# Second attention of a two-layer gated block: value products one tile behind their transpositions, first scores in front of the last down product

## What is computed

```python
x = x + tanh(g_xattn[0]) * _L0_xattn_ref(_layernorm(x), ctx_1024, W, b)          # phase A, one head
x = x + tanh(g_ffn[0])   * _L0_ffn_ref(_layernorm(x), ...)                       # phase B, 16 experts, top 4, shared expert
x = x + tanh(g_xattn[1]) * _L1_xattn_ref(_layernorm(x), ctx_1024, Wq, Wk, Wv, Wo, ...)   # phase C, 16 heads of 8
x = x + tanh(g_ffn[1])   * _L1_ffn_ref(_layernorm(x), ...)                       # phase D, 8 experts, top 2
...
    scores = jnp.einsum('bhqd,bhkd->bhqk', q, k)
    attn = jax.nn.softmax(scores, axis=-1)
    ctx = jnp.einsum('bhqk,bhkd->bhqd', attn, v)
    return ctx @ Wo.T + bo
```

## Time and profile before

| | |
|---|---|
| median of 3 runs | 322.72 us (322.35 to 323.2) |
| profiled execution, its own time | 322.1 us |
| span of the profile | 320.3 us |
| TensorE clock granted over the span | 0.987 of full speed |
| PE busy | 283.6 us, 89% |
| DVE busy | 237.1 us, 74% |
| ACT busy | 129.9 us, 41% |
| GpSimd busy | 87.7 us, 27% |

### The profile page before, as it was taken

The page is one execution under the profiler, slowest core; times in us unless marked ns, Lnnn a source line. Parts: engine busy times, 40 slices in busy tenths (PEclk is TensorE's granted clock), DMA queues, the critical chain, the costliest instruction groups (busy, mean ns, idle before and its releaser), DMA issues.

```text
span 320.3 us, 5453 instructions
## 1 busy us (share of the span) xinstructions
PE 283.6 (89%) x1646; PEld 210.7 (66%) x1646; DVE 237.1 (74%) x660; ACT 129.9 (41%) x275; POOL 87.7 (27%) x162
## 2 busy tenths in 40 slices
PE   6899689999899799488789789889889999999994
PEld 5688467666476465277677677768676676676661
DVE  2887979769989986557677686686748977778572
ACT  1587533242342332445454554554442332323320
POOL 8475310100650410733175165355110100100000
PEclk9999979999999999889999999999999999999999
DMA  6900164282341430000000000000024053231640
GB/s 225 337 21 0 37 222 148 54 242 67 102 156 46 132 123 33 0 2 0 2 1 2 0 2 3 0 0 3 0 86 158 25 190 75 106 125 35 210 154 33
DMA packets 15066, 25.26 MB, mean 79 GB/s; under 512 B 2341, under 2 KB 4339, under 8 KB 14835
## 3 DMA queue, kind: packets, MB, share of 16 engines
q1 hardware_dynamic: 12968, 23.88, 22.6%
q10 hardware_dynamic: 2072, 1.07, 1.2%
HBM read 22.98 MB, written 1.25 MB: 76 GB/s over the span
## 4 chain that ended last, share of the span: by engine, by line
PE 65%; issue 10%; DVE 9%; ACT 5%; DMA 5%; POOL 3%; SPq 2%; POOLq 0%; DVEq 0%; ACTq 0%
PE S L542 24%; PE Ybank L564 15%; PE Ybank L710 10%; PE S L687 2%; PE Tb L482 2%; DMA CR<-comb_rows 2%; DMA X<-in_x 2%; PE bank L697 2%; DVE xn L1059 2%; DMA comb_rows<-ct 1%; ACT pt L973 1%; PE Tb L674 1%; ACT PX L963 1%; SPq L307 1%; PE bank L580 1%
## 5 line engine op out<-in xcount | busy, mean ns | idle before, releaser
L858 ACT ACTIVATE sg<-S 128x512 f32<-128x512 f32 x64 | 38.0, 596 | 72.5 <-PE S L542 62.6
L1205 DVE TENSOR_TENSOR hb<-sg,CR 128x512 f32<-128x512 f32 x64 | 45.1, 705 | 13.0 <-issue 4.8
L337 POOL TENSOR_TENSOR rstd<-ve,mhalf 128x4 f32<-128x4 f32 x11 | 11.1, 1011 | 134.6 <-DVE ve L1052 134.6
L1198 DVE TENSOR_TENSOR sg<-sg,S 128x512 f32<-128x512 f32 x64 | 43.5, 680 | 5.7 <-ACT sg L858 3.5
L710 PE MATMUL Ybank<-VX,pt 128*128 128x128 f32 (+1 forms) x320 | 39.1, 277 | 6.7 <-ACT pt L973 6.7
L710 PEld LDWEIGHTS Ybank<-VX,pt 128*128 128x128 f32 (+1 forms) x320 | 37.1, 191 | 9.2 <-issue 9.1
L542 PE MATMUL S<-xh,WBH 128*128 128x512 f32 x64 | 33.3, 520 | 5.8 <-DVE sg L1198 3.0
L542 PE MATMUL S<-xh,UPH 128*128 128x512 f32 x64 | 36.1, 565 | 0.0
L564 PE MATMUL Ybank<-hb,W2T 128*128 128x512 f32 x64 | 33.0, 599 | 1.6 <-DVE hb L1205 1.6
L564 PE MATMUL Ybank<-hb,downw 128*128 128x512 f32 x64 | 33.0, 599 | 0.4 <-DVE hb L1205 0.4
L973 ACT ACTIVATE pt<-bank 128x512 f32<-128x512 f32 (+1 forms) x32 | 15.8, 494 | 35.4 <-PE bank L697 35.4
(11 more groups left out here) (164 smaller groups left out, 513.2 us busy)
## 6 DMA issues: line engine op xcount, KB each, us to landing
CR<-comb_rows SPq DMA_DIRECT2D x64, 128.0 KB, 3.0
CR<-comb_rows SPq DMA_DIRECT2D x32, 256.0 KB, 3.5
w13raw<-in_w SPq DMA_DIRECT2D x1, 1088.0 KB, 10.9
X<-in_x SPq DMA_DIRECT2D x4, 256.0 KB, 6.1
upraw<-in_up SPq DMA_DIRECT2D x4, 256.0 KB, 3.9
out_x<-X SPq DMA_DIRECT2D x4, 256.0 KB, 3.4
cT<-in_ctxT SPq DMA_DIRECT2D x2, 308.0 KB, 5.6
CN<-in_ctx SPq DMA_DIRECT2D x1, 616.0 KB
```

The lines of the kernel that those rows point to most:

```text
L858: A(sg[:, k % 2, :], Gb[k % 2][:], ACT.Silu).then_inc(m.s_done, 1)
L1198: V.tensor_tensor(sg[:, k % 2, :], sg[:, k % 2, :], Ub[k % 2][:], ALU.mult).then_inc(m.t2, 1)
L1205: V.tensor_tensor(hb[:, k % 2, :], sg[:, k % 2, :], CR[:, k % RING, :], ALU.mult).then_inc(m.h_done, 1)
```

## The change

1. PE runs mix(n−1) at the end of tile n, in place of mix(n). With it turn, project, normalize and final move from n−1 to n−2 on all engines. PE waits for final(n−2) (c_fin) in front of the extras and the mix in every tile, not only at t = 0 and 1. What is left over runs after tile 15: the gate and up products of D's unit 0, turn(14), mix(15), project(14), the products of unit 1, turn(15), project(15).
2. ACT runs copy 2 before exp(n+1, 0), not behind it.
3. scores(0) lies in front of the last down product of phase B: it waits for `m_gated` of unit 7 only (which frees the banks), not for `m_weighted`. `m_turn` of the last group lies in front of scores(1), and on DVE `m_update` in front of max(1, 0).
4. The statistics for the norm of group 1 are made in unit 3 of B's last group, not in unit 6. In phase C `norm_stats`, `inv_std` and `norm_apply` move from t = 3 to t = 2.

```diff
-                        add_bo(g)
-                    if t == GB - 1 and not last:
+                        add_bo(g)
+                    if t == 2 and not last:
                         inv_std(2 * NG + 3 + g)
                         norm_apply(2 * NG + 3 + g, (g + 2) % NG)
...
+            def c_begin(k):
                 if k == mB.units - 1:
-                    pe.wait_ge(mB.h_done, START + mB.units * (NG - 1) + mB.units)
+                    pe.wait_ge(mB.t2, NG * mB.units)
                     c_scores(0, 0)
...
+                    if n + 1 < NB:
+                        c_scores(*divmod(n + 1, GB))
                     c_transpose(g, t, 0)
...
+                    if n >= 2:
+                        c_turn(*divmod(n - 2, GB))
                     c_transpose(g, t, 1)
+                    if n >= 2:
+                        c_project(*divmod(n - 2, GB))
+                    c_transpose(g, t, 2)
+                    if n >= 2:
+                        pe.wait_ge(c_fin, START + n - 1)
...
+                    if n:
+                        c_mix(*divmod(n - 1, GB), n == 1)
...
-                    if stats_of is not None and k == m.units - 2:
+                    if stats_of is not None and k == (m.units - 2 if nm is not None else m.units - 5):
                         norm_stats(n + 1, stats_of)
```

More of the change, by code:

```diff
@@ L614, in m_body @@
                         m_route_T(nxt[1], nxt[2])
+                    if ahead:
+                        ahead(k)
                     m_down(m, g, k)
@@ L703, in c_mix @@
                 pe.wait_ge(c_norm, START + n)
-                if first and t == 0:
+                if first:
                     pe.wait_ge(mB.y_cp, START + NG)
@@ L723, in c_project, with c_body @@
                 mm(bWo, OTs[:], WXo[:], start=True, stop=True).then_inc(c_wo, 1)
-            def c_body(g, first, last):
+            def c_body(g, last):
                 for t in range(GB):
                     n = GB * g + t
[L729 to L733, removed]
+                    if n + 1 < NB:
+                        c_scores(*divmod(n + 1, GB))
                     c_transpose(g, t, 0)
@@ L740, in c_body @@
                         pe.wait_ge(route["vals"], mD.route_base + 1)
-                    if before:
-                        c_turn(*before)
+                    if n >= 2:
+                        c_turn(*divmod(n - 2, GB))
                     c_transpose(g, t, 1)
-                    if before:
-                        c_project(*before)
-                    if t == GB - 1 and last:
[L747 to L768, removed]
+                    if n >= 2:
[3 more added lines that the diff above has]
+                        pe.wait_ge(c_fin, START + n - 1)
+                    if t == 0:
+                        pe.wait_ge(x_done, START + 2 * NG)
+                        norm_T(2 * NG + 2 + g)
+                    if t == 1 and last:
+                        m_logits(mD, 0)
+                    if t == 1 and not last:
+                        c_query(g + 1)
+                    if t == GB - 1 and last:
                         m_route_T(mD, 0)
-                    if t or not first:
-                        c_mix(g, t, first)
+                    if n:
+                        c_mix(*divmod(n - 1, GB), n == 1)
             def c_ahead(k):
@@ L979, in c_turned, with c_body @@
                 A(OTs[:], bOT, ACT.Copy).then_inc(c_otc, 1)
-            def c_body(g, first, last):
+            def c_body(g, last):
                 for t in range(GB):
[L983 to L987, removed]
+                    n = GB * g + t
+                    c_copy(g, t, 0, n == 0)
+                    if n >= 2:
+                        c_turned(*divmod(n - 2, GB))
                     if t == GB - 1 and last:
                         m_route_tanh(mD, 0)
-                    c_copy(g, t, 1, first)
-                    if ahead:
-                        c_exps(*n1, 0)
-                    c_copy(g, t, 2, first)
-                    if t == 0 and not first:
+                    c_copy(g, t, 1, n == 0)
+                    c_copy(g, t, 2, n == 0)
+                    if n + 1 < NB:
+                        c_exps(*divmod(n + 1, GB), 0)
+                    if t == 0:
                         norm_hi(2 * NG + 2 + g, xh[:, slot(g + 1):slot(g + 1) + GT])
@@ L999, in c_body @@
                         m_route_copy(mD, 0)
-                    if ahead:
-                        c_exps(*n1, 1)
-                    if t == 0 and first:
-                        norm_hi(2 * NG + 2 + g, xh[:, slot(g + 1):slot(g + 1) + GT])
+                    if n + 1 < NB:
+                        c_exps(*divmod(n + 1, GB), 1)
             def c_ahead(k):
```

66 lines of the change are left out of this document (37 added, 29 removed).

## The result

The median of the changed kernel is 313.03 us (six runs, 312.47 to 316.27) against 322.85 for the kernel before in runs beside it (six, 321.52 to 323.2). The ratio on record is 0.9751, with a 95% interval of 0.9706 to 0.9797, which is a gain of 6.6 to 9.5 us. The quotient of the two medians is 0.9696, just outside the interval, so the −9.8 us of the medians is a little more than the interval bears out. The forecast was 313.7, with 311.2 to 317.2.

What follows compares the result with a forecast made beforehand. PE was taken as the main bound, 65% of the chain of waits. Steady tiles −3.5, seam −8.0 and tail +2.5 sum to −9.0 us: 313.1 against the profiled 322.1, 313.7 as median, range 311.2 to 317.2.

Steps and rivals of the forecast that it cites:

- The likeliest case: Whole kernel: the forecast itself, −9.0 us to 313.7, chance 0.59.
- Steady tiles: scores(3) to scores(15): wait for copy 2 goes, plain tile 5.6 us not 6.14; gain 3.5 us, ends 1.5 to 5.
- GpSimd's 0.1 per group: Steady tiles: added per group because GpSimd's keys at t = 3 fit with nothing to spare.
- Seam: Phase B to C: scores(0) and max start earlier, scores(3) at 141.5 not 149.54; gain 8.0 us, ends 5 and 9.
- Half clock at the seam: First rival, seam: scores(1), scores(2) and transpositions at half speed, 2 to 3 us more; 316 in all, chance 0.12.
- No stretch at half clock: Seam, forecast's sign: scores(1) near 131.8 with no PE wait over 1.5 us and the clock full.
- Tail: scores(15) to project(15): the owed work is paid here, 17.1 against 14.58; loss 2.5 us, ends 2 and 4.
- GpSimd's late keys: Rival, steady tiles: keys late with 0.05 us of room, 0.6 more per group; 315.5 in all, chance 0.12.
- The lag buys nothing: Rival, each tile: final or OTs ends as late as copy 2 did, mix stays at s + 3.74; 317.2, chance 0.08.
- The slower case: Rival, all 12 tiles: mix hangs on final; decides if final ends 0.85 us later; 325.7 at 1.0; chance 0.03.

Runs made afterwards that it cites:

- the seam alone: Kernel before with scores(0) ahead of the last down product, turn and `m_update` moved up, statistics in unit 3, no lag; 319.52 us, ratio 0.9884.
- without the wait for final: Changed kernel without PE's wait for c_fin in front of the mix at t = 2 and 3, tile 15 keeping it; 311.5 us, ratio 0.9622.
- the three edits at the end of the experiments: On the changed kernel, cumulatively: wait for final removed at t = 2 and 3 (311.5 us), keys before norm (308.98), turn first with statistics split (306.28).
- the lag alone: Changed kernel with the seam of B and C put back as before, the lag of the value products kept; 317.51 us, ratio 0.9838.
- B's statistics alone: Kernel before with only the statistics moved from unit 6 to unit 3 of B's last group; 320.61 us, ratio 0.9933.
- before with copy 2 first: Kernel before with only ACT's order changed, copy 2 in front of exp(n+1, 0); 322.88 us, ratio 0.996.
- the late norm: Changed kernel with phase C's norm statistics, `inv_std` and `norm_apply` put back to t = 3; 318.32 us, ratio 0.9873.
- the change once more: The changed kernel run again unedited; 313.09 us, ratio 0.9675.
- the one with copy 2 behind the exp: Changed kernel with ACT's order as before, exp(n+1, 0) in front of copy 2; 313.74 us, ratio 0.967.
- the keys first: Changed kernel without the wait for final at t = 2 and 3, and GpSimd spreading t = 3's keys before the norm; 308.98 us, ratio 0.9562.

## Why the prediction was right

**The sum.** −9.0 was forecast; −9.54 came by the stretches, −9.94 with a full clock at the seam of the changed kernel, and −9.8 by the medians. The likeliest case was the one that happened, and the mechanism of each term is in the rows. That the sum is within 1 us is in part luck: steady tiles and tail gave 1.2 more than forecast, the seam 0.2 to 0.6 less.

- **Steady tiles**: −3.5 forecast, −4.2 measured. A plain tile at 5.6 took 5.65 and 5.63. final is at s + 2.88 and not s + 2.81, and PE resumes 0.06 behind its end. The wait is there at t = 0, 2 and 3, 0.16 to 0.23 us and not 0.3. The tile at t = 1 was to stay at 6.35 and took 6.26; t = 0 took 5.98 against 6.1 by my terms. GpSimd's 0.1 per group didn't come: the tile at t = 3 took 5.63, though the keys were ready only 0.05 before its scores started. In sum 0.7 too little, 70.8 for 71.5, of which these keys are 0.3.
- **Seam**: −8.0 forecast, −7.36 and −7.80 measured. The chain was right link by link in the profile with a full clock: from scores(1) to scores(2) 4.21 for 4.2, from there to scores(3) 5.46 for 5.5. What was too short is its beginning: scores(0) comes 3.30 behind unit 7's first product, and I had 3.0. The 3.32 from its max to scores(1) held, and scores(1) was 7.52 behind unit 7 for 7.25. One part of this gain is not the new order. The forecast set a seam at full clock against a profile that had a half-clock episode in it, and took that episode for 1.8 us; by the seam alone it cost 1.2. So of the 7.80 about 6.6 is the order and 1.2 the clock.
- **Half clock at the seam**: here the forecast's statement failed in the profiled execution. "No stretch at half clock" was wrong, although no wait of PE is over 0.9 us; the first rival came in, with 0.44 in place of its 2 to 3. The argument against it was that a wait of 1.62 us had left the clock alone; one profile was too little for that, since the same code has profiles with the fall and without. In six of the nine profiles with the new seam the forecast's statement held. The Trainium skill, "TensorE: Matmul & The Clock Gate", its section "A second HAM failure mode: psum-queue depth-cycling", has the clock fall and rise again and again where matmul groups have frequent small idles between them. This profile agrees in part: small idles did go ahead of the fall. But it fell once, then the granted clock was 1.00 over all 70.77 us of tiles, each of which has one or two short waits.
- **Tail**: +2.5 forecast, +2.0 measured. mix(14) starts 2.78 behind the start of tile 15 (221.17), where I had 2.95; project(15) is at e + 11.05 for e + 11.5. The forecast's steps were each a little long, and the difference grew from 0.17 at mix(14) to 0.45 at project(15).
- **The rivals.** GpSimd's late keys cost PE nothing in the tiles of the change, but had no room left: without the wait for final PE waits 0.40 for them at each t = 3. "The lag buys nothing" fell to 0.23 against 0.75. The slower case would need final 0.85 later, and it is 0.07 later.

**How much of the 9.8 us is clock.** The runs' own mean clocks say that it isn't nothing. The kernel before had a median clock of 0.983 in the 45 runs that stood beside the experiments, the changed kernel 0.992 in its ten. In a straight line through the runs of each kernel, 0.01 of mean clock goes with 3.5 us of time before and 2.3 after. So, as an estimate, 2 to 3 us of the difference between the medians come with the clock, and some 7 to 8 us with the order of work. Whether the shorter waits are what raised the clock is not shown for the whole kernel.

**What the prediction didn't see.** It took the wait for final as part of the price of the lag; it is needed only where the tile has extras, and the experiments bring in 1.5 us for it. It counted the early norm at the 0.53 us per group that `norm_T` had waited; with the lag it is worth 1.36 at full clock (7.34 against 5.98). And it took OTs' 0.31 as given, though the order of two short operations on PE and ACT removes it.

## What to carry to other kernels

Moving a product one round later doesn't remove a wait but can hand it to the next producer, so price that one first: here PE's 0.75 for the copy became 0.23 for final. Sum the beginning, a round and the end apart, since a lag that gains in every round leaves a debt at the end (+2.0 here) and may gain most at the start (−3.9). When a wait goes, look for semaphores that are asked for out of habit, then for the short item that stands behind a long one in a queue: the three edits at the end of the experiments were together worth two thirds of the change again. And take a second profile before a fall of the clock is put down to an edit, or its absence to a cure: here one episode was as large as several of the edits.

## What the runs showed of the hardware

PE's clock fell in some profiles of one and the same code and not in others, and the length of the wait ahead went with how often. All four profiles with the wait of 3.37 us in front of scores(1) (the kernel before, the lag alone, B's statistics alone, before with copy 2 first) have half clock in the seam. Of the nine with the new seam, whose waits are at most 1.2 us, three have it. Behind the wait of 1.55 us of the late norm it came in two tiles of three. In the steady tiles of the other twelve profiles, where no wait of PE is over 0.75 us, it never came. With so few profiles that is a tendency and no rule.

When it comes is not fixed by the wait either. In front of scores(1) the kernel before and the lag alone both wait 3.37 us. Before, scores(1) itself ran at half clock (1.40 us). In the profile of the lag alone it ran at full speed, and the fall came some 1.4 us behind its start:

```profile
136.14 0.84 PE L689 MATMUL S<-KT,qq 32*128 32x308 f32 x16 [3.37 <-DVE PX L1336]
```

```profile
137.50:137.75 0.25, 0.25 (x4) 0.25 (x3) 0.25 (x1) 0.14 (x1) 0.25 (x1) 0.68 0.00 0
138.00:140.00 2.00, 1.64 (x9) 1.22 (x8) 1.49 (x3) 1.21 (x4) 0.42 (x1) 0.50 0.00 0
```

Waits of 0.78 and 0.88 went ahead of a fall in the first profile of the change, and had none behind them in four others with the same seam (the change once more, the one with copy 2 behind the exp, the one with no wait for final, the one with the late norm: 17.19 to 17.31 us, clock 1.00). With the keys first the fall came one step later, behind scores(2), and the seam took 18.36: PE issued transpositions, query and mix(0) there with no wait to cover them. So the price of one episode hangs on where it falls and how long it holds: 0.44 us where DVE's chain covered it, 1.2 in that case, 1.6 inside a tile (a t = 0 tile of 8.97 against 7.34). In the profile of B's statistics alone it held for some 10 us and cost about 3.2. The spread between runs of one kernel goes with the clock: of the 45 runs of the kernel before, those at 0.989 took 319.4 to 321.8 us and those at 0.977 or 0.978 took 323.5 to 326.1.

The short waits of the steady tiles repeat to the first decimal, on the other hand: PE's wait for OTs is 3.7 us over 12 tiles in the kernel before, in it with copy 2 first, and in the change with copy 2 last or with the late norm.
